# A perceiver kernel: first three units scored by banks with a spare bank for key tiles, the woven dilated norm applied by GpSimd, and another order for the last turned blocks

## What is computed

```python
def reference(x, ctx_2048, ...):            # x [2,128,256], ctx_2048 [2,2048,256]
    x = x + xattn0(layernorm(x), ctx_2048)  # 16 heads of 128: softmax(q k^T) v, Wo
    x = x + attn0(layernorm(x))             # cosine products of rotated keys and values
    x = x + ffn0(layernorm(x))              # 8 experts, the best two, softmax gate
    x = x + xattn1(layernorm(x), ctx_2048)  # 16 heads of 16, q, k, v and softmax rounded to 8 bits
    x = x + dilated(layernorm(x))           # segments of 64, every second row per head
    x = x + ffn1(layernorm(x))              # silu gate, block floating point (blocks of 32)
    return x
```

## Time and profile before

| | us |
|---|---|
| median of 3 runs | 679.12 (679.08 to 679.85) |
| the profiled execution | 679.84 |
| its span on the core | 678.5 |
| busy in the span: PE / DVE / ACT / POOL | 647.5 / 579.3 / 412.9 / 387.5 |
| granted TensorE clock, mean | 1.0 |

### The profile page before, as it was taken

The page is one execution under the profiler, slowest core; times in us unless marked ns, Lnnn a source line. Parts: engine busy times, 40 slices in busy tenths (PEclk is TensorE's granted clock), DMA queues, the critical chain, the costliest instruction groups (busy, mean ns, idle before and its releaser), DMA issues. The chain is left out here.

```text
span 678.5 us, 13895 instructions
## 1 busy us (share of the span) xinstructions
PE 647.5 (95%) x5089; PEld 410.0 (60%) x5089; DVE 579.3 (85%) x1038; ACT 412.9 (61%) x688; POOL 387.5 (57%) x499
## 2 busy tenths in 40 slices
PE   9899999999999999999999999998999989988897
PEld 7456676666676667677676657673456444544463
DVE  5998987897797898799989959888898899999865
ACT  4654455444455446556565433638998899899941
POOL 5886675656755655598986535345644643245401
PEclk9999999999999999999999999999999999999999
DMA  9656799757657678989976765779998999999910
GB/s 305 167 136 138 148 186 182 161 129 161 132 119 160 141 162 190 237 169 216 169 176 140 199 139 136 139 191 193 189 199 155 173 151 201 167 181 179 187 35 9
DMA packets 347827, 111.01 MB, mean 164 GB/s; under 512 B 313704, under 2 KB 344432, under 8 KB 347760
## 3 DMA queue, kind: packets, MB, share of 16 engines
q1 hardware_dynamic: 347760, 110.13, 78.7%
HBM read 31.97 MB, written 0.26 MB: 48 GB/s over the span
## 5 line engine op out<-in xcount | busy, mean ns | idle before, releaser
L1062 PE MATMUL psum<-c_nat,eT 128*128 128x256 f16 x1536 | 188.1, 273 | 0.9 <-ACT u_sb L1236 0.9
L1915 DVE TENSOR_REDUCE tops<-psum 128x1 f32<-128x512 f32 x256 | 158.8, 681 | 14.4 <-PE psum L1865 13.7
L1034 PE MATMUL psum<-cT,qk 128*128 128x512 f16 x744 | 165.6, 379 | 0.1
L1908 ACT ACTIVATE cT<-psum,bias,q_scale 128x1024 f16<-128x1024 f32 x128 | 153.4, 1204 | 16.9 <-PE psum L1865 16.1
L1062 PEld LDWEIGHTS psum<-c_nat,eT 128*128 128x128 f16 x1536 | 147.3, 98 | 24.1 <-issue 1.6
L1865 PE MATMUL psum<-kT,v_space 128*128 128x512 f16 x512 | 137.1, 380 | 10.7 <-DVE tops L1915 7.4
L1034 PEld LDWEIGHTS psum<-cT,qk 128*128 128x128 f16 x744 | 72.6, 98 | 82.3 <-issue 1.2
L1274 DVE TENSOR_REDUCE neg_max<-psum 128x1 f32<-128x2048 f32 x32 | 73.2, 2286 | 20.8 <-PE psum L1034 20.6
L1865 PEld LDWEIGHTS psum<-kT,v_space 128*128 128x128 f16 x512 | 44.5, 97 | 72.2 <-DVE tops L1915 36.1
L1262 DVE TENSOR_TENSOR e_lo<-e_all,e_hi 128x2048 f16<-128x2048 f32 x32 | 87.8, 2745 | 0.0
L1205 ACT ACTIVATE e_all<-psum,neg_max 128x2048 f32<-128x2048 f32 x32 | 63.0, 1970 | 16.7 <-DVE neg_max L1276 16.7
(11 more groups left out here) (289 smaller groups left out, 963.5 us busy)
## 6 DMA issues: line engine op xcount, KB each, us to landing
wvo_h<-in_L_xattn_Wv SPq DMA_DIRECT2D x30, 128.0 KB, 2.5
wvo_h<-in_L_xattn_Wo SPq DMA_DIRECT2D x30, 128.0 KB, 2.4
wqk_h<-in_L_xattn_Wq SPq DMA_DIRECT2D x28, 128.0 KB, 2.4
wqk_h<-in_wkT SPq DMA_DIRECT2D x28, 128.0 KB, 2.6
mx_land<-in_mx_weights SPq DMA_DIRECT2D x8, 384.0 KB, 4.0
v_space<-in_ctx SPq DMA_DIRECT2D x4, 512.0 KB, 5.9
cT<-in_ctx SPq DMA_DIRECT2D x2, 1024.0 KB, 8.1
c_nat<-in_expert_wT SPq DMA_DIRECT2D x2, 1024.0 KB, 6.3
```

Of the source, the lines that this page charges most:

```text
L1034: ins = pe.matmul(s_ps[:, n * 512:(n + 1) * 512], c.qk[:, u % 2, q_part, k, :], m.cT[:, b, c_part, 4 * n:4 * n + 4, k, :], start=(k, q_par ...
L1062: ins = pe.matmul(u_ps, c.eT[:, v % 2, e_part, j, :], m.c_nat[:, v // H0, c_part, j, :], start=(j, e_part, c_part) == (0, 0, 0), stop=(j, ...
L1908: act.activation(m.y[:, u % 2, q * CHUNK:(q + 1) * CHUNK], m.bank(second_place(u, q), 2), ACT.Exp, bias=m.bias[:, u:u + 1], scale=m.q_scal ...
L1915: dve.tensor_reduce(m.tops[:, n // NB, n % NB:n % NB + 1], m.bank(n % 3), AX.X, ALU.max, negate=True).then_inc(s["q_max"], 1)
```

## The change

1. `BY_BANK = 3`: the scores of units 0, 1 and 2 are made bank by bank, each with its own semaphore step, and DVE takes a maximum per bank (`dve_bank_top`, four instructions of 128x512 into `part_max`) and then the least of the four. Those of banks 0 and 1 of unit 0 stand in `dve_setup`. The counts of `scores` and `max` are adapted (`scored`, `limit_ready`).
2. `SPARE_KEYS = (1, 3)`: key tiles 1 and 3 go to bank 7, so they don't wait for the tile before.
3. `LATE_PIECE = 2`: POOL's two instructions of 128x2048 (L767) become four each of 128x512.
4. The norm of the woven dilated block (latent 0) is applied by POOL, at its slot "apply"; latent 1 keeps it on DVE.
5. `BACK_ACT = (5, 7)`: ACT copies the turned blocks 5 and 7, DVE 0 to 4 and 6. The three idle products move from behind block 7 to between the two halves of the last `attend`.

```diff
@@ dve_setup
     for h in range(2, 2 * GROUPS):
         turned(h)
+        if h == 2 * GROUPS - 2:
+            dve_bank_top(dve, m, c, s, 0, 0)
     dve_fold_key(dve, m, c, s, 1)
+    dve_bank_top(dve, m, c, s, 0, 1)
     dve.wait_ge(s["wkv_hi"], 1)
@@ pe_cross
         pe.wait_ge(s["exp"], u)
+        if u < BY_BANK:
+            for n in range(4):
+                for k in range(KD):
+                    for q_part, c_part in TERMS:
+                        ins = pe.matmul(m.bank(n), c.qk[:, u % 2, q_part, k, :], m.cT[:, b, c_part, 4 * n:4 * n + 4, k, :],
+                                        start=(k, q_part, c_part) == (0, 0, 0),
+                                        stop=(k, q_part, c_part) == (KD - 1, 1, 0))
+                ins.then_inc(s["scores"], 1)
+            return
@@ keys_values
-        else:
+        elif kt > SPARE_KEYS[-1]:
             pe.wait_ge(s["k_biased"], kt)
+        elif kt > 1:
+            pe.wait_ge(s["k_biased"], kt - 1)
@@ dve_cross
-            dve.wait_ge(s["scores"], u + 1)
+            if u < BY_BANK:
+                for n in range(0 if u else 2, 4):
+                    dve_bank_top(dve, m, c, s, u, n)
+            else:
+                dve.wait_ge(s["scores"], scored(u))
             if u > 1:
                 dve.wait_ge(s["exp"], u - 1)
-            dve.tensor_reduce(limit, s_ps, AX.X, ALU.max, negate=True).then_inc(s["max"], 1)
-            dve.wait_ge(s["max"], 2 * u + 1)
+            if u < BY_BANK:
+                dve.wait_ge(s["max"], limit_ready(u) - 2)
+                dve.tensor_reduce(limit, c.part_max[:, :], AX.X, ALU.min).then_inc(s["max"], 1)
+            else:
+                dve.tensor_reduce(limit, s_ps, AX.X, ALU.max, negate=True).then_inc(s["max"], 1)
+            dve.wait_ge(s["max"], limit_ready(u) - 1)
+def key_bank(m, kt):
+    return m.bank(7 if kt in SPARE_KEYS else 5)
+def dve_bank_top(dve, m, c, s, u, n):
+    dve.wait_ge(s["scores"], 4 * u + n + 1)
+    if u > 0 and n == 0:
+        dve.wait_ge(s["max"], limit_ready(u - 1))
+    dve.tensor_reduce(c.part_max[:, n:n + 1], m.bank(n), AX.X, ALU.max, negate=True).then_inc(s["max"], 1)
@@ pool_cross
             pool.wait_ge(s["late_hi"], u)
-            pool.tensor_tensor(m.c_nat[:, 1, 1, tiles, :], c.late_land[:, tiles, :], m.c_nat[:, 1, 0, tiles, :],
-                               ALU.subtract).then_inc(s["late_lo"], 1)
+            for n in range((u - 1) * LATE, u * LATE, LATE_PIECE):
+                tiles = slice(n, n + LATE_PIECE)
+                ins = pool.tensor_tensor(m.c_nat[:, 1, 1, tiles, :], c.late_land[:, tiles, :], m.c_nat[:, 1, 0, tiles, :],
+                                         ALU.subtract)
+            ins.then_inc(s["late_lo"], 1)
@@ dve_dilated, pool_dilated
     dve_norm(dve, m, s, b, NORM["dilated"], x_b, room)
-    yield at["apply"]
-    dve.wait_ge(s["ahead_in"], 48)
-    dve.wait_ge(s[f"root{b}"], NORM["dilated"])
-    dve.tensor_scalar(x.parity[:, :], a.row_mask, m.rstd[:, b:b + 1], None, ALU.mult).then_inc(sem, 1)
...
+    if not room.shared:
+        dilated_apply(dve, m, x, a, s, b)
     pool_norm(pool, m, s, b, NORM["dilated"], room)
+    if room.shared:
+        yield at["apply"]
+        dilated_apply(pool, m, x, a, s, b)
@@ pe_attention
-        if n == NB - 1:
-            pe.wait_ge(s["q_back_dve"], 3)
-            for _ in range(3):
-                pe_idle_product(pe, m, m.bank(2))
@@
             if u == UNITS and q < 2:
                 turn_quarter(NC // 2 + q)
+            if u == UNITS + 1 and q == 0:
+                for _ in range(3):
+                    pe_idle_product(pe, m, m.bank(2))
@@ act_attention, dve_attention
-    for n in range(BACK_DVE, NB):
+    for n in BACK_ACT:
         act.wait_ge(s["q_back"], n + 1)
-    for n in range(BACK_DVE):
+    for n in range(NB):
+        if n in BACK_ACT:
+            continue
```

More of the change, by code:

```diff
@@ L48 @@
 SPLIT = 6
+BY_BANK = 3
+SPARE_KEYS = (1, 3)
+LATE_PIECE = 2
 FIRST_PAIR = SPLIT - 4
@@ L70 @@
 SECONDS = ((1, 1), (1, 2), (2, 0), (2, 2))
-BACK_DVE = 7
+BACK_ACT = (5, 7)
 DG, DW = 4, 32
@@ L877, in act_fold_key @@
     if u > 1:
-        act.wait_ge(s["scores"], u - 1)
+        act.wait_ge(s["scores"], scored(u - 2))
     act.copy(flat(c.qk[:, u % 2, 0]), m.bank(4)[:, P:3 * P]).then_inc(s["qk_hi"], 1)
@@ L901, in pe_setup @@
     pe_turn_context(pe, m, c, s, 3)
-    pe_first_scores(pe, m, c, s, 0)
+    pe_first_scores(pe, m, c, s, 0).then_inc(s["scores"], 1)
     pe_turn_context(pe, m, c, s, 4)
     pe_turn_context(pe, m, c, s, 5)
-    pe_first_scores(pe, m, c, s, 1)
+    pe_first_scores(pe, m, c, s, 1).then_inc(s["scores"], 1)
     pe_query(pe, m, c, d, s, 1)
@@ L909, in pe_setup @@
     pe_fold_key(pe, m, c, d, s, 1, 1)
-    pe_first_scores(pe, m, c, s, 2)
+    pe_first_scores(pe, m, c, s, 2).then_inc(s["scores"], 1)
     pe_first_scores(pe, m, c, s, 3).then_inc(s["scores"], 1)
@@ L1019, in last_due, with scored, limit_ready @@
     return u - 3 if TURNED <= u - 3 < UNITS else None
+def scored(u):
+    return u + 1 + 3 * min(u + 1, BY_BANK)
+def limit_ready(u):
+    return 2 * (u + 1) + 4 * min(u + 1, BY_BANK)
 def pe_cross(pe, m, c, d, g, s, side):
@@ L1199, in act_cross @@
         if u < UNITS:
-            act.wait_ge(s["max"], 2 * u + 2)
+            act.wait_ge(s["max"], limit_ready(u))
             if u > 0:
@@ L1317, in dve_cross @@
             add_output(last)
+def key_bank(m, kt):
[5 more added lines that the diff above has]
+    dve.tensor_reduce(c.part_max[:, n:n + 1], m.bank(n), AX.X, ALU.max, negate=True).then_inc(s["max"], 1)
 def dve_key_tile(dve, m, d, s, kt):
-    ps, v_tile = m.bank(5), m.v_raw[:, kt, :]
+    ps, v_tile = key_bank(m, kt), m.v_raw[:, kt, :]
     heads = d.k_tmp.rearrange("p (h d) -> p h d", h=H1)
@@ L1422, in dve_value_inverses @@
     dve.wait_ge(s["v_scale_pe"], V_SCALE_PE["inverse"])
-    dve.wait_ge(s["scores"], H0)
+    dve.wait_ge(s["scores"], scored(H0 - 1))
     dve.tensor_copy(m.mix["v_inv"], ps[:, 0:D]).then_inc(s["v_scale_dve"], 1)
@@ L1924, in attend @@
         else:
-            pe.wait_ge(s["q_back_dve"], NB // 2 if half == 0 else BACK_DVE)
+            pe.wait_ge(s["q_back_dve"], NB // 2 if half == 0 else NB - len(BACK_ACT))
         if z == UNITS - 1 and half == 1:
-            pe.wait_ge(s["q_back_act"], NB - BACK_DVE)
+            pe.wait_ge(s["q_back_act"], len(BACK_ACT))
         if z in (H1, H1 + H1 // 2) and half == 0:
@@ L2155, in dve_dilated @@
     dve_norm(dve, m, s, b, NORM["dilated"], x_b, room)
-    yield at["apply"]
-    dve.wait_ge(s["ahead_in"], 48)
-    dve.wait_ge(s[f"root{b}"], NORM["dilated"])
-    dve.tensor_scalar(x.parity[:, :], a.row_mask, m.rstd[:, b:b + 1], None, ALU.mult).then_inc(sem, 1)
-    dve.wait_ge(sem, DIL_DVE["parity"])
-    for r in range(DIL):
-        ins = dve.tensor_scalar(x.mine.rearrange("p (n r d) -> p n r d", r=DIL, d=HD1)[:, :, r, :],
-                                x_b.rearrange("p (n r d) -> p n r d", r=DIL, d=HD1)[:, :, r, :],
-                                m.moments[:, b, 0:1], x.parity[:, r:r + 1], ALU.subtract, ALU.mult)
-    ins.then_inc(s[f"ln{b}"], 1)
+    if not room.shared:
+        dilated_apply(dve, m, x, a, s, b)
     yield at["own"]
@@ L2189, in dve_dilated, with dilated_apply @@
     dve.tensor_tensor(x_b, x_b, x.mine[:, :], ALU.add).then_inc(sem, 1)
+def dilated_apply(engine, m, x, a, s, b):
+    sem, x_b = s[f"dil_dve{b}"], m.x_res[:, b, :]
+    engine.wait_ge(s["ahead_in"], 48)
+    engine.wait_ge(s[f"root{b}"], NORM["dilated"])
+    engine.tensor_scalar(x.parity[:, :], a.row_mask, m.rstd[:, b:b + 1], None, ALU.mult).then_inc(sem, 1)
+    engine.wait_ge(sem, DIL_DVE["parity"])
+    for r in range(DIL):
+        ins = engine.tensor_scalar(x.mine.rearrange("p (n r d) -> p n r d", r=DIL, d=HD1)[:, :, r, :],
+                                   x_b.rearrange("p (n r d) -> p n r d", r=DIL, d=HD1)[:, :, r, :],
+                                   m.moments[:, b, 0:1], x.parity[:, r:r + 1], ALU.subtract, ALU.mult)
+    ins.then_inc(s[f"ln{b}"], 1)
 def dve_scores_less(dve, x, a, s, b, room, n):
@@ L2553, in act_feed, with pool_dilated @@
         middle_copy(act.copy, x, room, 3 + 2 * len(rounds) + h, h).then_inc(sem, 1)
-def pool_dilated(pool, m, s, b, room, at):
+def pool_dilated(pool, m, x, a, s, b, room, at):
     yield at["norm"]
     pool_norm(pool, m, s, b, NORM["dilated"], room)
+    if room.shared:
+        yield at["apply"]
+        dilated_apply(pool, m, x, a, s, b)
 def pool_feed(pool, m, x, s, b, room, at):
@@ L2617, in perceiver @@
                 pool_queries(pool, m, s, 1, room, queries), pool_output(pool, m, y, a, s, 0, 0, room, output),
-                pool_output(pool, m, y, a, s, 0, 1, room, output), pool_dilated(pool, m, s, 0, room, dilated),
+                pool_output(pool, m, y, a, s, 0, 1, room, output), pool_dilated(pool, m, z, a, s, 0, room, dilated),
                 pool_feed(pool, m, w, s, 0, room, feed), pool_output(pool, m, y, a, s, 1, 0, room, output_last)))
```

(2 more changed lines are left out.)

4 lines of the change are left out of this document (2 added, 2 removed).

## The result

The changed kernel takes **682.11 us** (median of 6 runs, 681.63 to 682.60), the kernel before on the same chip 679.37 (6 runs, 679.08 to 679.85). The ratio is 1.0039, 95% interval [1.0028, 1.0049]: slower by 2.7 us, beyond the 0.2% that a measurement of this kernel can tell. The forecast was 678.9, its range ended at 680.0. The profiled execution of after took 681.97 with a span of 680.6 at a granted clock of 1.0; the span grew by 2.1 us (678.5 before).

The account below looks back on a forecast made before the run. The prediction took a chain through DVE to bound the start until about 39 us, then a full PE, DVE leading again in the second attention, then a serial tail. Terms 0.45 - 0.42 - 0.23 = -0.20 gave 678.9 us; range 677.7 to 680.0.

Parts of the forecast that it names:

- the step that failed: Unit 0: maxima by banks cost DVE 0.40 us; the new order among the last turned tiles gives back 0.3.
- part 1: Units 0 to 2: banks, spare bank and POOL's pieces together make query 4 0.45 us later; bounds 0.4 gained, 0.8 lost.
- its 39.2: Units 1 to 3: the forecast is wrong if DVE's folded key of unit 3 comes before 39.2 us; 39.5 expected.
- Part 2: Woven block: with the norm on POOL, PE starts the product using it 0.42 us earlier; bounds 0.78 gained, 1.0 lost.
- Rival (b): Woven block: POOL applies the norm too late, PE and DVE wait; price 1.0 us, total 680.3 or 680.9; chance 0.08.
- signs of being wrong: Among them, in the woven block: the forecast is wrong if a second engine waits for POOL.
- Part 3: End: ACT's extra copy and the moved idle products start the last attend's second half 0.23 us earlier; bounds 0 and 0.5.
- All three: Rivals: blocking at the pieces goes away, 677.7 us (0.17); POOL's norm too late, 680.3 (0.08); change does nothing, 679.1 (0.23).

Follow-up runs that it names:

- E0: Not a run: the start of the exponentials of unit 0 on ACT in each profiled execution, from which distances such as that to query 4 are measured.
- maxima behind the weights: The changed kernel with all four bank maxima of unit 0 placed behind the low part of the key weights: 680.28 us, ratio 1.0008 to the kernel before.
- Without banks: The changed kernel without scores and maxima by banks, the rest of the change kept: 680.06 us beside 679.75 of the kernel before, ratio 1.0004.

## Why the prediction was wrong, point by point

**Unit 0, the step that failed.** "They stand among the last turned tiles, where the new order moves work ahead of a wait that DVE had there for ACT; by my reading of that stretch this gives back 0.3 of the 0.4, a choice, not a row". That size was nearly right. The wait is the one of `wkv` for ACT's high part of the same weights, which the kernel before shows in two rows: ACT ends at 15.79 + 1.08 = 16.87, and `wkv`, behind DVE's folded key, starts at 16.90.

```profile
15.79 1.08 ACT L970 ACTIVATE wkv<-e_all 128x1024 f16<-128x1024 f32 x1
16.39 0.41 DVE L884 TENSOR_TENSOR qk<-psum,qk 128x256 f16<-128x256 f32 x1
```

Four maxima behind the weights cost unit 0 0.23 us (5.75 against 5.52 from the turned tile to E0). With one or two of them ahead it is 0.04 to 0.05, once the stretch of `wkv` is taken off (5.56; 6.55 less 0.98; 7.52 less 1.95). So the order gave back some 0.2 us, and unit 0 would have cost 0.05 where 0.1 was forecast.

What failed is that this step stopped there: it counted the two maxima ahead of the low part of the key weights against a wait, and put at nothing what they do to that instruction. They push `wkv` by 0.99 us, across the start of POOL's 128x1024, and the price is 1.95 by the lock. The bounds of part 1 (-0.4 to +0.8) were made from the stretch of units 1 and 2 and the 0.3 of this step, and could not hold it. The prediction had the very mechanism, for the earlier trace rows, and used it at one place only.

**The rest of part 1.** Forecast +0.45 at query 4. Measured against E0, it is 18.65 - 18.86 = **-0.21** in after and -0.29 with the maxima behind the weights. The chain as described held: maxima 0.6 apart, at 30.61 behind `e_lo` and not earlier; PE's wait of 1.99 for the exponentials; three waits by turns. A unit of maxima by banks costs DVE 2.47 + 0.16 in place of 2.28 and a pause, 0.24 from E0 to the exponentials of unit 1 (10.81 against 10.57; 0.17 with the maxima behind the weights), where 0.4 was taken. The other difference is the phase: the pieces began 0.24 ahead of the tile's first instruction, the whole one, at 31.29, 0.12 behind it, so tile 2 got free of POOL earlier: 4.78 us to tile 3, and 5.22 before. Without banks the pieces began 0.14 behind it, and it took 5.17. That this phase would fall well was luck; no step of the prediction had it. The term had the wrong sign by this, within its bounds. One of the prediction's own signs shows it: the folded key of unit 3 stands 18.18 behind E0 in after and 18.38 before, which on the time of before is 38.89, ahead of its 39.2.

**A loss of 0.35 at unit 16** was in no term. Two rows of DVE in after:

```profile
244.64 0.16 DVE L1319 RECIPROCAL inv_sum<-row_sum 128x1 f32<-128x1 f32 x1 [0.28 <-issue]
...
244.91 3.76 DVE L1403 TENSOR_REDUCE v_top<-v_space 128x256 f32<-128x2048 f32 x1
```

DVE stands idle for 0.28 us ahead of the reciprocal, without a cause that the profile shows; the maximum over the values follows 0.35 later, and PE, which waits 0.41 for its result in before, waits 0.76. The gap is in the five kernels with maxima by banks (13.04 to 13.07 from the exponentials of unit 16 to those of unit 17) and in none of the seven without (12.70 to 12.74; the kernel before counted). So it comes with the banks, 200 us behind them, also where `wkv` is not stretched. Why is open; no run was made for it.

**Part 2.** Forecast -0.42, measured -0.03 in after and -0.09 alone. The start held: POOL's `parity` came right behind its step as forecast, took 0.32 (0.35 taken), and `mine` followed 0.10 later. Two sizes failed. The two instructions take 1.60 together, 0.80 each, where 0.65 was taken by columns from the earlier trace rows: 256 columns take 1.24 and 128, strided ones, take 0.80, so by an estimate from these two 128 columns more are worth 0.44 and some 0.36 of each instruction is fixed. And PE was not ready 0.78 earlier: it stands 0.31 ahead of the product in after, so it could have begun at 575.40, 573.31 in the time of before, 0.31 earlier than before. The two together leave nothing. Rival (b) named the right mechanism, PE waiting for POOL and DVE starving behind it (0.92 in after), and overpriced it; PE waiting for POOL in this block was one of the prediction's signs of being wrong.

**Part 3.** Forecast -0.23, measured -0.24 in after (1.85 against 2.09) and -0.25 alone. Every step of it held. The rows of PE in after:

```profile
650.16 0.55 PE L1981 MATMUL psum<-v_space,c_nat 128*128 128x16 f16 x16
650.57 0.81 PE L488 MATMUL psum<-kT,ident_fp 128*128 128x512 f16 x3
651.21 0.55 PE L1981 MATMUL psum<-v_space,c_nat 128*128 128x16 f16 x16
```

**The sum** by what was measured: +1.97 (unit 0, of it 1.95 by the lock) - 0.21 (units 1 and 2) + 0.35 (unit 16) - 0.03 (norm) - 0.24 (end) = +1.84, and DVE's last instruction is 1.83 later. The span differs by 0.3 more, behind that instruction, where only the output is written. The medians differ by 2.7, the profiled executions by 2.1: that of before lies 0.47 above the median of its six runs, that of after 0.14 below. The six runs of either kernel lie within 1 us of each other, and what makes up those 0.6 us is open. Without the lock the change is about even with the kernel before (ratio 1.0008, within 0.2%), which is what the forecast said of the rest; its -0.2 was not reached.

**The rivals.** All three looked at places where the change acts on purpose: pieces, norm, end. None was about an instruction that the change does not touch and only delays. That was the fourth way, and the one that came; the dearest price of a rival was 680.9, and the kernel takes 682.1.

## What to carry to other kernels

Where an instruction is put in front of others on an engine's queue, list every one that it delays up to the next wait, and for each of a kind that waited here (two inputs in SBUF, or a `tensor_scalar` on one SBUF tensor, which had the longest wait of all, 2.83 us) look at what the other engine of the pair starts in that interval; being 0.04 us behind it cost 1.95 us here, being 0.56 ahead nothing on that engine. Against such a wait, cutting the long instruction did little while the other side kept asking, here 2.87 in place of 2.83 us; moving it to a unit where something covers it gained 0.9 us of the chain and 0.19% of the time with one edited condition. An engine relieved of work on a chain that passes through two others gains only what the slower of these leaves: 0.78 us taken off DVE became 0.91 us of waiting for PE, which waited for POOL.
